# A decoder layer whose self-attention turns its probabilities two heads at a time

## What is computed

```python
# self-attention, x is the layer-normed input
def bitlinear(x, w, g):
    x_q = activation_quant(rmsnorm(x, g));  w_q = weight_quant(w)
    return jnp.einsum('btc,oc->bto', x_q, w_q)
Q = split_heads(bitlinear(x, wq, gq))
K = split_heads(bitlinear(x, wk, gk))
V = split_heads(bitlinear(x, wv, gv))
attn = softmax(jnp.einsum('bhtd,bhsd->bhts', Q, K) / math.sqrt(D_K))
out = jnp.einsum('bhts,bhsd->bhtd', attn, V)
return bitlinear(out.transpose(0, 2, 1, 3).reshape(B, T, C), wo, go)

x = x + self_attention(layernorm(x))
x = x + cross_attention(layernorm(x), ctx)
x = x + experts(layernorm(x))
```

## Time and profile before

| | us |
|---|---|
| median of 3 runs | 962.99 |
| lowest and highest | 962.37, 966.84 |
| the profiled execution | 964.96 |
| its span, first to last instruction | 963.2 |
| PE busy in the span | 787.8 (82%) |
| DVE busy | 632.4 (66%) |
| ACT busy | 535.6 (56%) |
| POOL busy | 386.0 (40%) |
| self-attention, first outputs (tile 0) to last (tile 15), start to start | 52.8 to 203.7 |

### The profile page before, as it was taken

How to read it: one execution, slowest core, us unless ns; L and a number is a source line. 1 busy time by engine, 2 the same in 40 slices (tenths; PEclk the granted TensorE clock), 3 DMA queues, 4 the chain that set the end, 5 groups by cost and what they waited for, 6 DMA issues and landing times. The chain is left out here.

```text
span 963.2 us, 29306 instructions
## 1 busy us (share of the span) xinstructions
PE 787.8 (82%) x11741; PEld 578.0 (60%) x11741; DVE 632.4 (66%) x1110; ACT 535.6 (56%) x1002; POOL 386.0 (40%) x445
## 2 busy tenths in 40 slices
PE   0599988864767999999999988862599999999992
PEld 0488878751323566566656656662477777777771
DVE  6788999553656899989999988667433333333330
ACT  1687878742545777676767664431155445445541
POOL 0231222320334555555555556300336555555542
PEclk9998999955998999999999989955799999999997
DMA  9110000000453444434243432092492222222223
GB/s 330 44 47 24 25 24 25 26 1 22 132 165 100 134 132 133 125 98 134 94 146 116 134 104 76 2 361 89 148 359 46 39 40 46 44 37 43 45 35 103
DMA packets 59402, 92.18 MB, mean 96 GB/s; under 512 B 6769, under 2 KB 39665, under 8 KB 59089
## 3 DMA queue, kind: packets, MB, share of 16 engines
q1 hardware_dynamic: 48048, 76.49, 23.9%
q0 software_dynamic: 7488, 10.23, 6.6%
q10 hardware_dynamic: 3744, 3.67, 1.1%
HBM read 63.36 MB, written 29.10 MB: 96 GB/s over the span
## 5 line engine op out<-in xcount | busy, mean ns | idle before, releaser
L1528 DVE SCALAR_TENSOR_TENSOR hid<-psu,hid 128x688 f32<-128x688 f32 x39 | 34.1, 875 | 146.3 <-ACT hid L1390 146.3
L1051 PE MATMUL xbank_qk<-arena 128*128 128x512 f16 x384 | 97.7, 392 | 20.8 <-DVE q_hl L960 15.8
L1146 PE MATMUL xbank_a<-arena,x_o 128*128 128x256 f16 x768 | 95.7, 275 | 2.8 <-DVE x_sb L999 1.7
L1390 ACT ACTIVATE hid<-psg 128x688 f32<-128x688 f32 x39 | 29.0, 744 | 117.3 <-PE psu L1597 117.3
L1612 PE MATMUL fbank<-arena,hidT 128*128 (+1 forms) x663 | 82.8, 273 | 0.8 <-ACT f_y L1410 0.8
L1146 PEld LDWEIGHTS xbank_a<-arena,x_o 128*128 128x128 f16 x768 | 72.6, 98 | 18.0 <-DVE x_o L970 7.8
L857 ACT ACTIVATE sqq<-xbank_qk 128x512 f32<-128x512 f32 x64 | 38.2, 597 | 78.0 <-PE xbank_qk L1051 78.0
L1597 PE MATMUL psg<-wgu,f_xT 128*128 x468 | 75.0, 310 | 4.0 <-ACT f_xT L1397 2.2
L1597 PE MATMUL psu<-wgu,f_xT 128*128 x468 | 74.6, 309 | 0.0
L1612 PEld LDWEIGHTS fbank<-arena,hidT 128*128 128x128 f16 (+1 forms) x663 | 62.9, 97 | 15.4 <-issue 9.2
L1051 PEld LDWEIGHTS xbank_qk<-arena 128*128 128x128 f16 x384 | 33.0, 99 | 63.2 <-DVE q_hl L960 23.9
(11 more groups left out here) (257 smaller groups left out, 1955.1 us busy)
## 6 DMA issues: line engine op xcount, KB each, us to landing
arena<-in_wx SPq DMA_DIRECT2D x51, 256.0 KB, 3.7
wgu<-w_hl SPq DMA_DIRECT2D x8, 1376.0 KB, 9.0
ao<-key_norms SPq DMA_DIRECT2D x64, 128.0 KB, 3.2
w_hl<-cT SPq DMA_DIRECT2D x26, 256.0 KB, 2.1
w_hl<-x_pair SPq DMA_DIRECT2D x25, 256.0 KB, 3.4
ao<-in_wx SPq DMA_DIRECT2D x16, 256.0 KB, 3.0
w_hl<-ao SPq DMA_DIRECT2D x16, 256.0 KB, 2.1
arena<-w_hl SPq DMA_DIRECT2D x8, 384.0 KB, 8.8
```

What stands on the lines that cost most here:

```text
L1051: last = nc.tensor.matmul(bank_q, wq[:, a, k, f:f + D2], hT[:, g, b * NCH + k, :], start=(j == 0), stop=(j == len(terms) - 1))
L1146: last = nc.tensor.matmul(acc[t // 2][:, (t % 2) * C:(t % 2 + 1) * C], o_hl[h % 2][:, a, at:at + P], wvo[:, b, e, :], start=(e == 0 and j ...
```

## The change

Probabilities are turned by full 128x128 transposes. Two neighbouring heads of `sp` are 128 columns; one transpose puts head 2k on rows 0 to 63 and head 2k+1 on rows 64 to 127, with both sequences side by side in the columns. A part is 4 transposes in place of 16 products. ACT copies as many values as before.

The outputs of an even head then need the values of both sequences on rows 0 to 63, those of an odd head on rows 64 to 127. One sequence lies there already in `vb`, the other comes from a new tile `vs`, a copy with the halves exchanged. SP makes it with two transfers for each tile (64 rows of 1088 bytes each), from SBUF to SBUF. PE's outputs wait for them, and they go over the even heads first and then, after a wait for the last of the even half (`even_done`), over the odd heads. The products are of the same number and size.

SP's list is now in the order of the steps: the load of raw piece n stands in odd step 2n-3, and the two transfers of tile t+2 in step t, the latter after a wait for the outputs of tile t. `turned_hidden` goes from DVE to ACT, between the copy of part 0 of the probabilities and `value_high`. Four constants that nothing read are gone: 448 columns of 128 rows in fp32, 229 KB of the first loads.

```diff
-IDENT, ONES, SAMEB, POS, PICK0, PICK1, BEFORE, CONSTS = 0, 128, 256, 384, 448, 576, 704, 832
+IDENT, ONES, BEFORE, CONSTS = 0, 128, 256, 384
...
+                def swapped_values(i):
+                    sp_.wait_ge(vb_done, i + 1)
+                    need(sp_, o_done, i - 1)
+                    for b in range(2):
+                        sp_.dma_start(vs[i % 2][S * b:S * b + S, :, :], vb[i % 3][S - S * b:P - S * b, :, :]).then_inc(vs_in[i % 2], 16)
+
+                for t in steps:
+                    if t % 2 and 2 <= (t + 3) // 2 < NSPLIT:
+                        load_piece((t + 3) // 2)
+                    if tile(t + 2):
+                        swapped_values(t + 2)
...
+                    if pair(t, 8) is not None:
+                        turned_hidden(pair(t, 8))
                     if pair(t, 2) is not None:
                         value_high(pair(t, 2))
...
-                    if pair(t, 8) is not None:
-                        turned_hidden(pair(t, 8))
...
-                    for n in range(8):
-                        for b in range(2):
-                            rows = slice(S * b, S * b + S)
-                            last = nc.tensor.matmul(pt[rows, n * S:(n + 1) * S], sp[i % 2][rows, 8 * part + n, :], cst[rows, IDENT + S * b:IDENT + S * b + S], start=True, stop=True)
+                    for n in range(4):
+                        last = nc.tensor.transpose(pt[:, n * P:(n + 1) * P], sp[i % 2][:, 8 * part + 2 * n:8 * part + 2 * n + 2, :].rearrange("p h s -> p (h s)"), cst[:, IDENT:IDENT + P])
                     last.then_inc(p_done, 1)
...
-                    for n in range(H1):
-                        for b in range(2):
-                            rows = slice(S * b, S * b + S)
-                            last = nc.tensor.matmul(g1[rows, n * VW:(n + 1) * VW], pT[rows, n, :], vb[i % 3][rows, n, :], start=True, stop=True)
+                    pe.wait_ge(vs_in[i % 2], (i // 2 + 1) * 32)
+                    for side in range(2):
+                        rows = slice(side * S, side * S + S)
+                        if side:
+
+                            pe.wait_ge(even_done, i + 1)
+                        for n in range(side, H1, 2):
+                            for b in range(2):
+                                v = vb[i % 3] if b == side else vs[i % 2]
+                                last = nc.tensor.matmul(g1[S * b:S * b + S, n * VW:(n + 1) * VW], pT[rows, n // 2, S * b:S * b + S], v[rows, n, :], start=True, stop=True)
+                        if not side:
+                            last.then_inc(even_done, 1)
```

More of the change, by code:

```diff
@@ L128, in attention @@
         mx = [sb(f"mx{i}", [P, H1], F32) for i in range(2)]
-        pT = sb("pT", [P, H1, S], F32)
+        vs = [sb(f"vs{i}", [P, H1, VW], F32) for i in range(2)]
+        pT = sb("pT", [P, H1 // 2, P], F32)
         rden = sb("rden", [P, H1], F32)
@@ L157, in attention @@
         raw_in = [sem(f"a_raw_in{i}") for i in range(2)]
+        vs_in, even_done = [sem(f"a_vs_in{i}") for i in range(2)], sem("a_even_done")
         in_w, in_c, in_g, in_vo = sem("w_loaded"), sem("const_loaded"), sem("g_loaded"), sem("wv_wo_loaded")
@@ L202, in _, with load_piece @@
                         sp_.dma_start(cst[:, :], dram["consts"]).then_inc(in_c, 16)
-                for n in range(NSPLIT):
+                def load_piece(n):
                     need(sp_, low_done, n - 1)
                     sp_.dma_start(raw[n % 2][:, :], splits[n][0]).then_inc(raw_in[n % 2], 16)
+                for n in range(2):
+                    load_piece(n)
                     if n == 1:
@@ L298, in turned_probs @@
                     need(act, o_done, i)
-                    nc.scalar.copy(pT[:, 8 * part:8 * part + 8, :].rearrange("p h n -> p (h n)"), pt[:, :]).then_inc(pT_done, 1)
+                    nc.scalar.copy(pT[:, 4 * part:4 * part + 4, :].rearrange("p h n -> p (h n)"), pt[:, :]).then_inc(pT_done, 1)
                 def squares(j):
@@ L329, in h_high, with turned_hidden @@
                     nc.scalar.copy(hp[:, :, 0, :], h[:, :, :]).then_inc(hh_done, 1)
+                def turned_hidden(j):
+                    act.wait_ge(ht_done, j + 1)
+                    at = j % 2 * 2 * P
+                    nc.scalar.copy(hT[:, j // 2, :, at:at + 2 * P].rearrange("p j (a n) -> p a j n", a=2),
+                                   g2[:, :].bitcast(F16).rearrange("p (a j n) -> p a j n", a=2, n=P)).then_inc(hT_done, 1)
                 def split_high(n):
@@ L485, in hidden @@
                         nc.vector.tensor_scalar(h[:, a, :], x_sb[:, 2 * j + a, :], mv_o[:, j, a, 0:1], rstd_h[:, j, a:a + 1], ALU.subtract, ALU.mult).then_inc(h_done, 1)
[L487 to L491, removed]
                 def value_low(n):
@@ L1645, in constants @@
     import numpy as np
-    p, m, s = np.arange(P)[:, None], np.arange(P)[None, :], np.arange(S)[None, :]
-    parts = [p == m, p >= 0 * m, p // S == m // S, p % S == s, p == m % S, p == S + m % S, p < m]
+    p, m = np.arange(P)[:, None], np.arange(P)[None, :]
+    parts = [p == m, p >= 0 * m, p < m]
     c = np.concatenate([np.asarray(x, np.float32) for x in parts], axis=1)
```

## The result

The forecast was 959.7 us, about as fast as before. The changed kernel is slower: a median of 978.9 us (975.6 to 985.4, four runs) beside 964.2 for the kernel before, a ratio of 1.015 with a 95% interval from 1.012 to 1.019. The profiled execution is the slowest of its four, 985.39 us, 20.4 more than the profiled one of before; its clock over the whole span is 0.875, and that of the three others 0.881 to 0.887, against 0.914 to 0.928 in the executions of the kernel before beside the experiments.

The account below looks back on a forecast made before the run. No one engine bounds self-attention: PE, DVE and ACT are 76 to 90% busy. Gain -7.2, ACT's copy +2.9, start -0.5, clock +1.5 sum to -3.3 us: 961.7 profiled, 959.7 median; range 952 to 971.

Parts of the forecast that it names:

- the clock, +1.5 us: Self-attention: more PE idle time raises the 1.2 GHz share by half; PE loses 7.4 us, a fifth through: +1.5 us.
- the clock stays low: Rival, self-attention: half the time at half clock makes PE the bound, 969 us; above 1040 at worst; chance 0.19.
- The gain of -7.2 us: Self-attention: seven tenths of DVE's 10.3 us of waits for PE's outputs, keys and scores fall away, -7.2 us.
- The transposes: Turning the probabilities: 0.45 us a part at 2.4 GHz, down from 1.08, freeing PE by 0.63 us a part.
- The outputs: Self-attention outputs on PE: halves cost no more than before, -0.3 to 0 us; sign in the profile, 1.9 to 2.3 us.
- outputs on the same rows run in series: Rival, self-attention outputs: products sharing rows run one after the other, doubled outputs +2.0 us a tile, 976 us; chance 0.08.
- The drain: Between the halves of a tile's outputs: waiting for `even_done` empties PE's array once a tile, 0.2 us.
- ACT's copy, +2.9 us: Turned hidden states, self-attention steps and tail: copying on ACT instead of DVE, 2.7 + 0.55 - 0.65 + 0.33 = +2.9 us.
- The start, -0.5 us: Kernel start: 229 KB less ahead of three quarters of x, shortening DVE's wait for the last, -0.5 us.
- The transfers: Self-attention: later raw-piece loads and SBUF exchanges of values stay covered, both 0 us; an uncovered exchange costs 3.7 us a tile.
- signs named in advance: Self-attention profile: DVE's PE waits under 5 us, `value_high` near 10, tile 15 outputs near 200.5; wrong if clock under 0.8.
- the rival at 969: The rival the clock stays low, in self-attention, worked out at half the time at half clock: 969 us, chance 0.19.

Follow-up runs that it names:

- e7: Kernel before, eight of the sixteen products that turn a part left out from the second tile on: 972.0 us, ratio 1.010.
- e13: Changed kernel with eight unused transposes more behind each tile's outputs: 972.6 us, ratio 1.0075.
- e16: Kernel before, half of the turning products left out from the second tile on, eight unused transposes behind each tile's outputs: 968.2 us, ratio 1.004.
- e8: Kernel before with one wait more, for the first half of a tile's outputs to be written: 968.2 us, ratio 1.005.
- e4: Kernel before with ACT instead of DVE copying the turned hidden states: 967.7 us, ratio 1.003.
- e2: Changed kernel with every transpose issued twice: 971.6 us, ratio 1.009.
- e3: Changed kernel with the probabilities turned by the sixteen 64x64 products of before, a wait after eight, into the new layout: 983.3 us, ratio 1.018.
- e18: Changed kernel, hidden-state copy back on DVE, eight unused transposes between scores and part 1 in steps without value weights: 977.1 us, ratio 1.012.
- e21: Kernel before with eight unused transposes between scores and part 1, in the steps without value weights: 973.2 us, ratio 1.008.
- e17: Kernel before with four unused transposes behind each tile's outputs: 965.9 us, ratio 1.000.
- e10: Changed kernel with eight unused 128x128 products behind each tile's outputs: 977.8 us, ratio 1.014.

## Why the prediction was wrong

**The step that failed is the clock, +1.5 us.** I let the share at 1.2 GHz grow from 18% by half as much again, to 27%, and let a fifth of what PE loses through to the end. The share went to 62%, which by the same working is 36 us of PE and not 7.4, and self-attention ended 17.7 us later although PE had less to do. A fifth of 36 us is 7, so both factors were too small (the 17.7 us hold the cost of copy and drain too). The reason I gave, 1.1 us more of idle time a tile, was the right one: e7 takes that much work away and nothing else, and e13 puts nearly as much back. What I had not seen is that the clock answers to that very idle time so strongly that it takes back all that was saved and more. The rival on record, *the clock stays low*, had the path and the size: PE becomes the bound where the share s is above 0.4, and a tile then takes 7.7/(1 - s/2) us. With s = 0.62 that is 11.2; the reciprocals say 11.06. Had I put s = 0.62 into it, fifteen steps would have given +17 us and the program 984, on the base of the profiled execution, beside the 985.4 us of the execution from which the 0.62 is read. What it did not have is the reason, since it took the transposes for what keeps the clock low. I gave it a chance of 0.19 and worked it out at s = 0.5. The range ended at 971.

**The gain of -7.2 us did not come, and not because of the clock alone.** It was given its price while the clock stood, as an amount of its own. With the clock nearly held, in e13, DVE's waits for outputs and scores are 6.1 and 5.3 us, not under 5 together, and the ratio of 1.0075 is just that of copy and drain in the kernel before (1.0056, 1.003 to 1.008), with nothing left over for a gain. e16 is no better in the kernel before: half of the turning and the unused work, the clock at 0.87, and 1.004. But none of these runs has both the work gone and the clock held, so what the transposes would be worth then was not measured. No kernel that was tried has both.

**What held.** The transposes: 0.46 us a part between starts at 2.4 GHz, as taken.

```profile
121.09 0.63 PE L554 MATMUL bank_pt<-cst,sp 128*128 128x128 f32 x4 [0.95 <-ACT pT L317]
121.55 0.44 PE L581 MATMUL bank_q<-zT,w_pad 128*128 128x128 bf16 x5
```

The outputs: from the first of tile 5 to the next group,

```profile
114.01 0.23 PE L616 MATMUL bank_g<-vb,pT 64*64 64x17 f32 x1
...
116.23 0.55 PE L554 MATMUL bank_pt<-cst,sp 128*128 128x128 f32 x3
```

is 2.22 us for 64 records and the drain, inside the forecast's 1.9 to 2.3. So the rival *outputs on the same rows run in series* is out, and so is, for this form, the rule of the Trainium skill ("TensorE: Matmul & The Clock Gate", Part 3) on which it stood: here the weight loads of products on the same rows, next to each other, start 0.01 us apart, while products on these rows run.

```profile
114.56 0.21 PE L616 MATMUL bank_g<-vb,pT 64*64 64x17 f32 x1
...
114.59 0.14 PEld L616 LDWEIGHTS bank_g<-vb,pT 64*64 64x64 f32 x1
114.60 0.14 PEld L616 LDWEIGHTS bank_g<-vs,pT 64*64 64x64 f32 x1
```

The drain was sized at 0.2 us. Its rows:

```profile
114.92 0.50 PE L616 MATMUL bank_g<-vs,pT 64*64 64x17 f32 x2
...
115.19 0.13 PEld L616 LDWEIGHTS bank_g<-vs,pT 64*64 64x64 f32 x1 [0.17 <-PE bank_g L616]
```

From the last even start to the first odd one it is 0.27 us, against 0.06 otherwise: 0.2 a tile. But it lies in front of DVE's wait for the outputs, and e8 puts it at 4.8 us (2.8 to 6.8) for sixteen, where 0.2 us in fifteen steps at seven tenths had made 2.1.

ACT's copy, +2.9 us: e4 measured 3 (0.6 to 5.4). The start, -0.5 us, came as taken, DVE reaching the last of its statistics at 15.79 instead of 16.36:

```profile
15.79 1.41 DVE L408 BATCH_NORM_STATS2 stats<-x_sb 128x6 f32<-128x256 f32 x4 [0.16 <-DMA x_sb<-in_x]
```

It was then lost in the first tile. The transfers cost nothing that the profile shows: an exchange lands in 2.0 us, the last six raw pieces in 3.8 to 4.2 (median of each pair), and neither ACT nor PE waited for them.

```profile
vs<-vb SPq DMA_DIRECT2D x32, 68.0 KB, 2.0
```

Of the signs named in advance, four spoke against me at once: the clock under 0.8, DVE's waits for PE at 23.3 us and not under 5, those for `value_high` at 6.5 and not near 10, and the outputs of tile 15, which start at 219.56 us:

```profile
219.56 0.29 PE L616 MATMUL bank_g<-vb,pT 64*64 64x17 f32 x1 [0.68 <-ACT pT L317]
```

**Transposes and the clock.** I had weighed the sentence of the Trainium skill that the full clock does not engage for transposes ("TensorE: Matmul & The Clock Gate", Part 4) beside the rival at 969. The side was right, but the measurements here speak against the rule: in the rows above fp32 transposes run at 2.4 GHz, e2 and e13 bring the clock back with nothing but more of them (0.912 over the runs in both, against 0.881), and e7 loses it without one. What the transposes did is be short.

What stays open: what of TensorE's work the clock goes by. The runs vary its amount and its place, and e3, e18 and e21 don't follow the amount alone, but no run separates the rest. Open too is the state in which tile 0 is met: the stretch at half clock ahead of about 55 us differs between profiles of kernels whose instructions are the same up to there. Nor was it tried to spare the drain by writing the odd heads to a bank of their own, since all banks are in use.

## What to carry to other kernels

Where the granted clock is under 1.00 and other engines make TensorE wait, idle time of TensorE may not be free, as here: before you price a saving on it, ask whether the clock will fall, and work out the tile at the share of half clock from which TensorE becomes the bound. Two small edits tell: a part of the work left out, and some unused work put in (here behind each tile's outputs, and not where it delays what the others wait for); if the first makes the kernel slower and the second costs nothing, as in e7 and e17, expect little of a faster form of that work. Where a rival's price hangs on one unknown, as here on the share at half clock, work it out at the far end too before giving it its chance.

## What was not expected of the hardware

- Less work made TensorE slower at an unchanged program otherwise (e7: -1.1 us a tile, clock 0.91 to 0.79, 1% slower), and useless work made a kernel faster (e13: +0.93 us a tile, clock 0.69 to 0.87, 6 us).
- The clock fell 0.3 us into a wait of 1.38 us (the changed kernel, tile 0) and held through one of 0.94 (e10) and one of 1.82: the length of the wait at hand did not decide it.
- TensorE was busy for 154.9 of 165 us at a mean granted clock of 0.69.
- A plain fp32 product of 128x128 leaves two records and takes 0.24 us at 2.4 GHz, an fp32 transpose of the same size one record and 0.115 us.
- A drain of 0.17 us of standing, once a tile, cost 4.8 us in sixteen tiles (2.8 to 6.8), DVE's wait for the outputs growing by 4.1.
- The granted clock of a stretch reads 1.00 up to the first change that the trace has noted, though PE's rows show half speed there: in the kernel before up to 46.05 us, in e13 up to 54.47.
